# Attention places of one or two query tiles, all key groups upward but the last

## What is computed

```
q, k, v = x@Wq.T, x@Wk.T, x@Wv.T        # 32 query heads, 8 key heads, 32 wide
qr, kr = apply_rope(q), apply_rope(k)
draft = qr @ kr.T + causal_mask
_, draft_indices = top_k(draft, 205)     # per query row and head
scores = qr @ kr.T / sqrt(32) + causal and "kept by top_k" masks
out = softmax(scores) @ v @ Wo.T
```

## Time and profile before

| | us |
|---|---|
| median of three runs (4492.38 to 4498.23) | 4497.68 |
| the profiled execution | 4494.27 |
| its span | 4492.4 |
| TensorE busy in the span | 3420.3 (76%) |
| VectorE | 3192.9 (71%) |
| ScalarE | 2687.5 (60%) |
| GpSimd | 1996.8 (44%) |

### The profile page before, as it was taken

One profiled execution on the slowest core, in us unless ns is written; L12 is line 12 of the kernel. 1 busy time (PEld: TensorE's weight loads), 2 busy tenths in 40 slices (PEclk: granted clock), 3 DMA queues, 4 the chain that ended last, 5 costly groups with the idle time before them and its releaser, 6 DMA issues. The chain is left out here.

```text
span 4492.4 us, 55609 instructions
## 1 busy us (share of the span) xinstructions
PE 3420.3 (76%) x15624; PEld 1589.6 (35%) x15864; DVE 3192.9 (71%) x6121; ACT 2687.5 (60%) x4577; POOL 1996.8 (44%) x5916
## 2 busy tenths in 40 slices
PE   5888883678768767787886668888767788885998
PEld 3444441333333323333332323333323333332444
DVE  3565555888888658888885788888658888882333
ACT  1111113788668657886875778888657888782111
POOL 0211113555345656543565655556655555572000
PEclk9888886889889878898997788999878899997999
DMA  2111112000010010000100100010010000002121
GB/s 97 51 59 58 50 55 47 15 12 9 6 19 12 17 30 12 12 9 6 22 15 20 25 12 9 9 19 12 19 28 12 12 9 9 9 17 74 71 75 52
DMA packets 221531, 123.99 MB, mean 28 GB/s; under 512 B 187940, under 2 KB 206628, under 8 KB 221092
## 3 DMA queue, kind: packets, MB, share of 16 engines
q1 hardware_dynamic: 221092, 119.36, 9.5%
HBM read 76.28 MB, written 42.99 MB: 27 GB/s over the span
## 5 line engine op out<-in xcount | busy, mean ns | idle before, releaser
L892 PE MATMUL banks<-pT,v_sb 128*65 128x512 f32 x2176 | 1183.3, 628 | 37.5 <-ACT oT L996 36.2
L981 ACT ACTIVATE pT<-banks 128x512 f32<-128x512 f32 x1088 | 637.2, 592 | 649.5 <-PE banks L864 643.6
L840 PE MATMUL banks<-k_sb,q_sb 128*128 128x512 bf16 (+3 forms) x1188 | 477.5, 402 | 329.4 <-DVE sc L1145 296.3
L1168 DVE MAX8 near<-keys 128x8 f32<-128x256 f32 (+14 forms) x480 | 653.4, 1361 | 16.5
L972 ACT ACTIVATE junk<-sc,t_all 128x256 fp8e4<-128x256 f32 (+14 forms) x480 | 599.2, 1249 | 33.3 <-DVE sc L1145 31.5
L972 ACT ACTIVATE junk<-sc,tiny 128x256 fp8e4<-128x256 f32 (+14 forms) x480 | 595.5, 1246 | 36.2 <-DVE sc L1153 35.8
L972 ACT ACTIVATE junk<-sc,tt 128x256 fp8e4<-128x256 f32 (+14 forms) x480 | 598.4, 1247 | 1.9 <-POOL tt L1037 1.2
L842 PE MATMUL banks<-k_sb,q_sb 96*128 96x512 bf16 (+3 forms) x1280 | 505.1, 405 | 76.3 <-DVE sc L1145 70.5
L1145 DVE TENSOR_SCALAR_CACHE_REDUCE sc<-banks 128x1024 f32<-128x1024 f32 (+7 forms) x512 | 501.2, 980 | 55.5 <-PE banks L845 30.6
L1153 DVE TENSOR_SCALAR sc<-sc,tt 128x256 f32<-128x256 f32 (+14 forms) x480 | 360.5, 814 | 236.5 <-POOL tt L1058 236.1
L858 PE MATMUL banks<-q_sb,k_sb 128*128 128x512 bf16 x940 | 383.9, 408 | 128.9 <-DVE fb L1322 113.3
(11 more groups left out here) (248 smaller groups left out, 5353.8 us busy)
## 6 DMA issues: line engine op xcount, KB each, us to landing
q_sb<-scratch_qk SPq DMA_DIRECT2D x896, 32.0 KB, 1.9
scratch_qk<-parts SPq DMA_DIRECT2D x16, 960.0 KB, 3.7
a_x<-in_x SPq DMA_DIRECT2D x16, 512.0 KB, 4.2
scratch_x<-a_x SPq DMA_DIRECT2D x16, 512.0 KB, 2.9
scratch_attn<-o_sb SPq DMA_DIRECT2D x128, 64.0 KB, 1.6
c_xn<-scratch_attn SPq DMA_DIRECT2D x16, 512.0 KB, 3.6
c_x<-scratch_x SPq DMA_DIRECT2D x16, 512.0 KB, 4.5
out<-c_x SPq DMA_DIRECT2D x16, 512.0 KB, 2.6
```

Source lines behind the costliest of these rows:

```text
L840: nc.tensor.matmul(r_slot(n)[:, j:j + wj], q_sb[:, p % QS, 0, h, :], k_sb[:, group[p] % 2, 0, col:col + wj], start=True, stop=False)
L892: nc.tensor.matmul(psum[0:VP, 6, :], v_sb[:, group[p] % 2, kb, :], pT[:, n % PTS, :], start=(kb == 0), stop=(kb == blocks[p] - 1)).then_in ...
L981: nc.scalar.activation(pT[:, tn % PTS, :], psum[:, 4 + n % 2, :], ACT.Exp, scale=SCALE)\
L1168: v.max(near[:, h, :], z).then_inc(sm["key"], 1)
```

## The change

Tiles 0 and 1, 2 and 3, 4 and 5, 6 and 7 of a group become one place each (its tiles are called segments); tiles 8 to 15 stay places of their own. A group has twelve places for sixteen, the phase 96 for 128. Groups 0 to 6 all go up, the last goes down. Small operations run once per place, on up to 8 columns (64 where there were 32); GpSimd's three conversions of a count take two operations for a pair. Wide operations still run per tile and head. In a pair of (0,1) only tile 1 is searched. `PTS` goes from 4 to 3, `oT` gets two buffers, `keys` one for two, query buffers are 9 for 5 (of tiles). Of a pair at j-2, the first tile is normalised right after the first evacuation of step j, and turned back on TensorE before the first score unit. The branch is entered per tile.

```diff
-PLACE = [(g, i) for g in range(HKV) for i in (range(TILES) if g % 2 == 0 else range(TILES - 1, -1, -1))]
+SETS = [(0, 1), (2, 3), (4, 5), (6, 7)] + [(i,) for i in range(8, TILES)]
+PLACE = [(g, tiles) for g in range(HKV) for tiles in (SETS if g + 1 < HKV else SETS[::-1])]
+COLS = 2 * REP
-QS, SCS, PTS = 5, 3, 4
+QS, SCS, PTS, OTS = 9, 3, 3, 2
...
-        units[j] = [("T", j - 1, kb) for kb in range(blocks[j - 1])] if here(j - 1) else []
+        units[j] = [("T", s, kb) for s in segs[j - 1] for kb in range(blocks[s])] if here(j - 1) else []
...
-        keys = sb("keys", [P, 2, S])
+        keys = sb("keys", [P, S])
...
-        oT = sb("oT", [VP, REP * P])
+        oT = sb("oT", [VP, OTS, REP * P])
...
+                        if not seen:
+                            while len(back) > 1:
+                                turn_back(back.pop(0))
...
+                def signed_sum(into, p, k, factor):
+
+                    x = sgn[:, p % 3, k, cols[p]]
+                    if len(hunted[p]) == 1:
+                        link(gp.tensor_scalar(into, x, factor, b.tab[:, tile_of[last_seg[p]], TAB_COUNT:TAB_COUNT + 1],
+                                              ALU.mult, ALU.add))
+                    else:
+                        link(gp.tensor_scalar(into, x, factor, None, ALU.mult))
+                        link(gp.tensor_tensor(by_tile(into), by_tile(into), of_tiles(p, TAB_COUNT), ALU.add))
...
                     if here(j + 2):
                         evacuate(j + 2, 0)
-                    if searching(j):
+                    if here(j - 2):
+                        for s in segs[j - 2][:-1]:
+                            normalise(s)
+                    if here(j):
                         directions(j)
                     for h in range(REP):
-                        if searching(j):
-                            nearest(j, h)
+                        if here(j):
+                            for s in hunted[j]:
+                                nearest(s, h)
```

More of the change, by code:

```diff
@@ L811, in _ @@
                     if j >= 2:
[L812 to L816, removed]
+                        for s in segs[j - 2]:
+                            store(s)
+                    if here(j + ahead):
+                        for s in segs[j + ahead]:
+                            load_q(s)
+                    g, n = divmod(j, len(SETS))
+                    if n == 3 and 1 <= g and g + 1 < HKV:
                         load_k(g + 1)
@@ new lines, in values, with turn_back @@
+                            if s:
+                                pe.wait_ge(sm["ot"], s)
+                        nc.tensor.matmul(psum[0:VP, 6, :], v_sb[:, group[s] % 2, kb, :], pT[:, n % PTS, :],
+                                         start=(kb == 0), stop=(kb == blocks[s] - 1)).then_inc(sm["pv"], 1)
+                def turn_back(s):
+                    pe.wait_ge(sm["ot"], s + 1)
+                    if s:
+                        pe.wait_ge(sm["norm"], s)
+                    pe.wait_ge(sm["flg"], min(place[s] + 2, N))
@@ L946, in _ @@
-                        if not back and seen == min(LAG + 2, blocks[p]):
-                            turn_back(j - 2)
-                            back = True
-                            if held is not None:
-                                flags(held)
+                        values(blocks_before[s] + kb - LAG)
+                        if kb + 1 == min(LAG, blocks[s]):
+                            values(blocks_before[s] - 1)
+                        if back and kb + 1 == min(LAG + 2, blocks[s]):
+                            turn_back(back.pop(0))
@@ L998, in _ @@
                 act.wait_ge(sm["fill"], 1)
                 for j in range(-2, N + 2):
[L1000 to L1004 removed]
+                    counts = [(s, k, h) for p, k in ((j, 2), (j + 1, 1), (j + 2, 0)) if here(p)
+                              for s in hunted[p] for h in range(REP)]
@@ L1005, in _ @@
+                    first = REP * len(hunted[j]) if here(j) else 0
+                    todo = []
+                    for kind, s, kb in units[j]:
+                        todo.append((kind, s, kb))
+                        if kind == "T" and s and kb + 1 == min(LAG, blocks[s]):
+                            todo.append(("O", s - 1, 0))
+                    if j == N + 1:
+                        todo.append(("O", len(place) - 1, 0))
                     for c in counts[:first]:
@@ new lines, in nearest @@
+                def nearest(s, h):
+                    p, n = place[s], key_no[s, h]
+                    z = keys[:, 0:width[s]]
+                    if n:
+                        dve.wait_ge(sm["key"], n)
+                    link(v.tensor_scalar(z.bitcast(I32), sc[:, p % SCS, h, offset[s]:offset[s] + width[s]].bitcast(I32), 2,
+                                         flip[:, column(s, h):column(s, h) + 1], ALU.logical_shift_right, ALU.bitwise_xor))
+                    v.max(near[:, column(s, h), :], z).then_inc(sm["key"], 1)
```

589 lines of the change are left out of this document (317 added, 272 removed).

## The result

| | us |
|---|---|
| before, median of 4 runs | 4495.03 |
| changed kernel, median of 4 runs (4681.93 to 4697.22) | 4692.76 |
| ratio, 95% interval | 1.044 [1.041, 1.047] |

The account below looks back on a forecast made before the run. Each step is bound by its busiest engine plus a loss: 761 + 2814 + 352 + 70 + 24 + 14 = 4035 against 4092.7, 58 earlier, less 4 at the end; 4497.7 - 54 = 4443 us, range 4370 to 4535.

Parts of the forecast that it names:

- Three pT buffers for four: ScalarE's exponentials wait for the value matmul behind their own scores: 0.15 us a step, 14 us (0 to 95).
- rival 2: Tight coupling: third pT buffer late every step, 1.0 to 1.5 us each; 4571 us, decides from 0.72 a step; chance 0.20.
- second search: The closer second search in four steps, dependent on the data: stays at 70 us beyond the normal loss.
- front normalise: VectorE waits, after its first evacuation, for TensorE to turn back a pair's first tile: 24 us (0 to 60).
- the 3.7 us of a broad step: Loss of every new step beyond its busiest engine: 95 x 3.7 = 352 us, against 529 in the kernel before.
- terms of order: All-upward groups put tile 15's score units beside a nearly empty VectorE in (0,1): busiest engines 2814 us, 73 more.
- Width costs nothing: GpSimd's small operations take 0.2 to 0.3 us on 4 or 32 columns; a pair's three extra cost 0.8, hidden.
- The price for GpSimd slowed beside VectorE: Judging operations at 1.07 us in pair steps beside busy VectorE: about 1 us in 8 steps, sum 8 us higher.
- `keys` in one buffer: The next key write waits some 0.05 us for a finished search, hidden by evacuation except in pairs; priced nothing.
- The flag: VectorE's wait for the flag at a step's end: 5.4 us in all before, left hidden, priced nothing.
- The three signs of a wrong prediction: Steps 9 to 13 growing a microsecond or more; exponentials waiting hundreds of microseconds on value matmuls; (0,1) exceeding 40 us.
- Rival 3: TensorE's clock stays 0.70 through (6,7) and tile 8 after idle narrow steps: 69 us more, 4512; chance 0.05.

Follow-up runs that it names:

- the zigzag: Group order of the kernel before, alternately up and down; the changed kernel put back to it: 4625.51 us, +134.9; with four pT and one oT buffer too: 4477.87 us, -19.0.
- a_pts4o1: The changed kernel with four pT buffers for three and one oT buffer for two: 4540.15 us, ratio 1.010.
- the early counts: The changed kernel with ScalarE's second counts for the next place all ahead of the step's exponentials: 4654.77 us, ratio 1.035.

## Why the prediction was wrong

The miss is 252 us (+198 for -54), and two terms of the sum carry it: about 134 to 140 the buffer, about 106 the loss in steps with pairs.

- **Three pT buffers for four: 14 us predicted, 134 to 154 measured.** This is the step that failed. 134 in the kernel before (1.05 us for each of 128 steps), 148 in the changed one upward (49.5 to 197.7), 154 in the zigzag (-19.0 to +134.9), 1.6 us for each of 95 steps. The working compared TensorE's slack of 2.9 us with ScalarE's 0.6 and 2.1, so it asked only whether TensorE would stall. It left out what ScalarE itself loses: it idles until the value matmul, and its counts stand in the same queue. Nor did TensorE's slack hold: its wait for exponentials rose from 38 us to 150, and to 144 in the kernel before. Even the upper end, 95 us, was too low. This is rival 2 by its mechanism, its size (1.0 to 1.5 a step) and the point from which it decides (0.72); it had 0.20. Its time of 4571 is still 122 us short, for the pairs lose as well. The measured time lies outside every range that the prediction gave. Its text said where to look, the 641 us that exponentials wait: an engine that waits 442 times for another has no slack against it.
- **The loss of a paired step: 3.7 us taken, 8.7 measured** in the mean of (2,3), (4,5) and (6,7), second search left out, by the prices of the prediction and the marks of the run with four buffers (`a_pts4o1`). With four buffers the marks are 3366 us apart: less 2814 and 70, the loss is 482 in 95 steps, 5.1 each, where 3.7 and 24 us for normalise gave 376. It is not spread evenly. In the sixth group of that run (2,3) takes 34.7 us, (4,5) 39.7 and (6,7) 38.4 against priced 27.2, 29.1 and 31.7: 24.8 us lost in three steps, against 11.1 by the average. Over all eight groups these steps lose 208 us, 119 more than at 3.7; (0,1) loses 2.3 each, 10 less in all, and the single tiles 21 more. Of these 130 us, 24 were foreseen as front normalise. So "each losing the 3.7 us of a broad step" is wrong for pairs: a pair has two tiles' second counts in a row on ScalarE, and VectorE can begin neither tile's differences before the last one. The repairs size the parts in the changed kernel: counts 40, front normalise 25, branch 8 at most and not clear of noise. They don't add up in a strict sense, and what (6,7) loses was not taken apart. That the late second counts hold up the differences is shown for one step and by the early counts; for the rest of the loss the cause stays open.
- The terms of order held as sums: +133 by prices, +132.5 measured in the kernel before; 73 by prices in the changed kernel, 63 (three `pT`) and 68.5 (four) measured. That 132.5 meets 133 so closely is in part luck: in the inner groups tile 0's step comes out 10 us under its price and tile 1's 16 to 19 over it.
- The front normalise was priced 24 and gives 25 when moved. The first mark at 759.6 for 761, the end 7 us for 4, and the second search stayed at four long steps, 52 to 55 us, 70 beyond their neighbours: right.
- "Width costs nothing" on GpSimd was nearly right: 1583 us busy in the phase against 1846 and 1450 predicted, and in the step read through its own 5 us are not what makes `tt` late; its exception stands below. The price for GpSimd slowed beside VectorE did not come: the judging operation L1170 took 0.56 us in pairs and 0.85 in single tiles. `keys` in one buffer showed no wait of its own.
- The flag was left hidden; VectorE waited 104 us for it, mostly where TensorE's work fills the step, and a second branch read per pair was not in the sum at all.
- The three signs of a wrong prediction: steps 9 to 13 of groups 1 to 5 grew, against the same steps of the kernel before in upward order, by 2.0, 2.7, 0.6, 1.4 and 0.5 us in the median (from 29.3, 31.6, 31.9, 35.0, 36.3), so by a microsecond or more in three of five; exponentials waited 952 us with value matmuls as releaser; (0,1) stayed under 40. The second came whole, the first in part, the third not.
- One reading was loose: in tiles 10 to 13 the three engines lie 3.2, 2.8, 2.5 and 2.0 us apart by the prediction's own list, not within 2.
- Rival 3, the clock, did not occur: after steps at 0.77 and 0.73 the granted clock is 0.90 in (6,7) and 0.94 in tile 8. The rule that activity releases the clock (the Trainium skill, "TensorE: Matmul & The Clock Gate", Part 1) agrees with these rows.

Not tried: four `pT` with two `oT`; LAG = 2 in the kernel before with four `pT`; the pairs with two `keys` buffers; the port between VectorE and GpSimd by itself.

## What to carry to other kernels

Before taking a buffer from a ring, write down which instruction frees it and what stands ahead of that on its engine: where the freeing instruction comes behind one's own input, the ring costs a wait in each turn, and moving it one place forward (here LAG 3 to 2) gave back 148 and 167 us, at least as much as the fourth buffer. Slack must be counted on both sides of a handover, and for an engine with several duties in one queue also for the duty behind. Merging steps saves their fixed losses only if the small results in them still come early: price the merged step by when its last small result is ready, not by the average loss.

## What the runs showed that was not expected

GpSimd's power operation has the clearest growth with columns among its small operations. Groups of the changed kernel (lines by form; busy, mean ns, idle before):

```profile
L1119 POOL TENSOR_TENSOR pw_b<-pw_b,minus 128x4 f32<-128x4 f32 x72 | 83.8, 1164 | 5.6
...
L1119 POOL TENSOR_TENSOR pw_b<-pw_b,minus 128x8 f32<-128x8 f32 x24 | 40.4, 1685 | 1.9
```

1.16 us on four columns and 1.69 on eight, on the way to `tt`; most single records are 1.04 and 1.67. Others of that chain (0.24 us for L1112 and 0.20 for L1124 on eight columns, above) take what they take on four, while the selectors' operations on 64 columns grow a little (L1159: 0.25 us on 32, 0.33 on 64). By these records the power costs a pair 0.6 us more, at most 15 us in 24 pairs searched on eight columns, an estimate. Reading two flags and branching twice leaves VectorE idle for 3.68 us ahead of the mark, with no releaser. And a lag shortened from three units to two, which gives the exponential less time before its value matmul needs it, was 14 us faster than before even with one buffer fewer: TensorE's wait for exponentials was 47.1 us there, 38.4 before. Why it is faster no run shows.
